# The gather of a deformable convolution: all row units sent by DMA over two queues, weights by one clamp in place

## What is computed

```python
def _deform(x, ow, ob):
    off = (_conv(x, ow, 1) + ob[None, :, None, None]).reshape(B, C, 2, H, W)
    py = jnp.clip(yy + off[:, :, 0], 0.0, H - 1)
    px = jnp.clip(xx + off[:, :, 1], 0.0, W - 1)
    y0, x0 = floor(py), floor(px);  y1, x1 = min(y0 + 1, H - 1), min(x0 + 1, W - 1)
    wy, wx = py - y0, px - x0
    return v00*(1-wy)*(1-wx) + v01*(1-wy)*wx + v10*wy*(1-wx) + v11*wy*wx
h = _deform(x, ow1, ob1);  h = _bn(_conv(h, w1, 0), g1, b1, m1, v1)
h = _deform(h, ow2, ob2);  h = _bn(_conv(h, w2, 1), g2, b2, m2, v2)
h = _deform(h, ow3, ob3);  h = _bn(_conv(h, w3, 0), g3, b3, m3, v3)
```

## Time and profile before

| | |
|---|---|
| Three runs | 5919.41, 5877.91, 5885.14 us; median 5885.14 |
| Profiled execution, span | 5921.8 us (no separate time beside it is on record) |
| TensorE busy, instructions | 5032.9 us (85%), 30592 |
| VectorE | 3610.3 us (61%), 4317 |
| ScalarE | 1856.8 us (31%), 2899 |
| GpSimd | 1464.4 us (25%), 1828 |
| SyncE's queue of the 16 DMA engines | 271640 packets, 533.13 MB, 36.3% |

### The profile page before, as it was taken

One profiled execution on the slowest core, in us unless ns is written; L12 is line 12 of the kernel. 1 busy time (PEld: TensorE's weight loads), 2 busy tenths in 40 slices (PEclk: granted clock), 3 DMA queues, 4 the chain that ended last, 5 costly groups with the idle time before them and its releaser, 6 DMA issues. The chain is left out here.

```text
span 5921.8 us, 79668 instructions
## 1 busy us (share of the span) xinstructions
PE 5032.9 (85%) x30592; PEld 2727.3 (46%) x30592; DVE 3610.3 (61%) x4317; ACT 1856.8 (31%) x2899; POOL 1464.4 (25%) x1828
## 2 busy tenths in 40 slices
PE   4877877876999799997998995999999967986987
PEld 2333333324777677766776772222222233232222
DVE  6888878885666566653222223767677765653764
ACT  2222222202222122210000003667677743641750
POOL 0222222230000000002001002555555543442540
PEclk7888888867999899998999997889799887777987
DMA  1000000001000000002211216889899968857962
GB/s 30 15 15 22 22 22 22 15 15 72 15 15 8 22 1 14 15 19 100 68 61 65 75 50 153 205 196 211 181 219 216 210 171 174 185 121 137 215 172 92
DMA packets 272018, 538.25 MB, mean 91 GB/s; under 512 B 167976, under 2 KB 169576, under 8 KB 264728
## 3 DMA queue, kind: packets, MB, share of 16 engines
q1 hardware_dynamic: 271640, 533.13, 36.3%
HBM read 419.75 MB, written 113.25 MB: 90 GB/s over the span
## 5 line engine op out<-in xcount | busy, mean ns | idle before, releaser
L1436 POOL TENSOR_SCALAR g_kw<-g_kw 128x512 f32<-128x512 f32 x1536 | 947.0, 641 | 904.3 <-ACT g_kw L1422 666.3
L1422 ACT ACTIVATE g_vw<-ps,l_index 128x512 f32<-128x512 f32 x1536 | 970.0, 685 | 409.5 <-PE ps L1478 409.4
L1455 DVE SCALAR_TENSOR_TENSOR g_prod<-g_vw,ps 128x1024 f32<-128x1024 f32 x768 | 902.7, 1217 | 271.4 <-PE ps L1493 270.8
L1296 PE MATMUL ps<-o_pad,o_ow 128*128 128x512 f32 x3456 | 851.8, 408 | 8.4 <-DVE o_pad L822 7.7
L1478 PE MATMUL ps<-g_coord,l_spread 80*128 80x512 f32 x1920 | 743.2, 489 | 125.2 <-DMA g_coord<-coords 125.1
L1093 PE MATMUL ps<-l_pair,l_w 128*128 128x512 f32 x3072 | 779.8, 403 | 0.0
L1478 PEld LDWEIGHTS ps<-g_coord,l_spread 80*128 80x128 f32 x1920 | 343.2, 213 | 906.3 <-ACT g_vw L1422 679.6
L1296 PEld LDWEIGHTS ps<-o_pad,o_ow 128*128 128x128 f32 x3456 | 656.8, 191 | 197.9 <-DVE o_pad L822 7.9
L1093 PEld LDWEIGHTS ps<-l_pair,l_w 128*128 128x128 f32 x3072 | 575.7, 191 | 156.4 <-issue 29.4
L1422 ACT ACTIVATE g_kw<-ps,l_index 128x512 f32<-128x512 f32 x384 | 264.3, 688 | 1176.3 <-PE ps L1478 1162.1
L1493 PE MATMUL ps<-g_kw,g_img 32*32 32x512 f32 x12288 | 508.9, 687 | 126.2 <-DVE g_prod L1455 100.0
(11 more groups left out here) (247 smaller groups left out, 4737.7 us busy)
## 6 DMA issues: line engine op xcount, KB each, us to landing
g_rows<-whole SPq DMA_DIRECT2D x1536, 192.0 KB, 4.9
coords<-o_parts SPq DMA_DIRECT2D x32, 1024.0 KB, 4.0
g_coord<-coords SPq DMA_DIRECT2D x96, 256.0 KB
l_x<-xcur SPq DMA_DIRECT2D x16, 1024.0 KB, 6.1
coords<-o_parts SPq DMA_DIRECT2D x32, 512.0 KB, 5.6
g_img<-dense SPq DMA_DIRECT2D x96, 128.0 KB, 4.4
gathered<-g_res SPq DMA_DIRECT2D x48, 256.0 KB, 4.7
l_xn<-in_x SPq DMA_DIRECT2D x8, 1024.0 KB, 5.0
```

The lines of the kernel that those rows point to most:

```text
L1296: ins = nc.tensor.matmul(ps[:, lo:lo + HALF], ow[:, a, kk, tap, y, k * P:(k + 1) * P], padded_rows(pad[:, m, c, kk], j, tap), start=(n == ...
L1422: nc.scalar.activation(to, bank(a % RING), ACT.Relu, bias=index[:, 0:1]).then_inc(sem("ring_read"), 1)
L1436: nc.gpsimd.tensor_scalar(part, part, 1.0, 0.0, ALU.min, ALU.max).then_inc(sem("clamped"), 1)
L1455: nc.vector.scalar_tensor_tensor(prod[:, n % PB, 2 * half:2 * half + 2, :].rearrange("p r n -> p (r n)"), vw[:, n % VB, 2 * half:2 * half ...
```

## The change

In each turn the y positions of all four channels of a unit are sent by DMA, 8 KB a partition, so the fifth spread matmul, its ScalarE pass and the loads of row coordinates go. Blocks 0 and 1 are sent from SyncE's queue, blocks 2 and 3 from GpSimd's. There are five buffers for rows, and a buffer is free when the row matmuls that read it have ended. The weights are made in place: instead of clamp(y - i + 1, 0, 1) a partition holds clamp(y, i - 1, i), with both limits from a column `clamp`, on GpSimd for channel 0 and on VectorE for the others. The constant i - 1 that is left over in each weight is made up for in image row 0, whose weight is always 1: `ramp_base` computes what has to stand there in the offset blocks. The positions of y no longer need splitting.

```diff
+def ramp_base(nc, link, out, rows):
+    link(nc.vector.tensor_reduce(out, rows[:, 0:SIDE - 1, :].rearrange("p y w -> p w y"), AX, ALU.add))
+    return nc.vector.scalar_tensor_tensor(out, rows[:, SIDE - 1, :], -float(SIDE - 2), out, ALU.mult, ALU.add)
@@ Coordinates.vector
         link(stt(pos, off, bias, grid, ALU.add, ALU.add))
-        link(ts(pos, pos, 0.0, float(SIDE - 1), ALU.max, ALU.min))
+        clipped = ts(pos, pos, 0.0, float(SIDE - 1), ALU.max, ALU.min)
+        if columns is None:
+            return clipped
@@ build_gather
-        KB, VB, PB, SB = 3, 2, 2, 3
+        VB, PB, SB = 2, 2, 5
+        def send_row(eng, q, r, half):
+            s, j, g = quads[q]
+            lo = r * SIDE + 4 * g
+            eng.dma_start(rows[r * SIDE:(r + 1) * SIDE, q % SB].rearrange("p c n -> p (c n)"),
+                          whole[s, j, lo:lo + 4].rearrange("q n -> (q n)").partition_broadcast(SIDE))\
+               .then_inc(sem(f"{half}_rows_sent{q % SB}"), 16)
@@ SyncE
-                        sp.wait_ge(sem("sent_relu"), q - SB + 1)
-                    for r in (0, 2, 1, 3):
+                        sp.wait_ge(sem("rows_summed"), q - SB + 1)
+                    for r in range(2):
+                        send_row(sp, q, r, "even")
-                def load_rows(s):
@@ GpSimd
-                    for c in range(4):
-                        ...
-                        nc.gpsimd.tensor_scalar(part, part, 1.0, 0.0, ALU.min, ALU.max).then_inc(sem("clamped"), 1)
+                nc.gpsimd.memset(coord[CM:CROWS, :, :, :].bitcast(F32), 0.0).then_inc(sem("coord_zero"), 1)
+                pool.wait_ge(sem("coord_zero"), 1)
+                for q in range(SB):
+                    send_odd(q)
+                for q in range(Q):
+                    await_rows(pool, q)
+                    part = rows[:, q % SB, 0, :]
+                    nc.gpsimd.tensor_scalar(part, part, clamp[:, 0:1], clamp[:, 1:2], ALU.max,
+                                            ALU.min).then_inc(sem("first_clamped"), 1)
+                    if q + SB - 2 >= SB and q + SB - 2 < Q:
+                        send_odd(q + SB - 2)
@@ VectorE
+                def clamp_rows(q):
+                    await_rows(dve, q)
+                    part = rows[:, q % SB, 1:4, :].rearrange("p c n -> p (c n)")
+                    nc.vector.tensor_scalar(part, part, clamp[:, 0:1], clamp[:, 1:2], ALU.max,
+                                            ALU.min).then_inc(sem("rest_clamped"), 1)
@@ build_offsets_1, for each image and channel half
+                            link(ramp_base(nc, link, base[:, m % 2, k, :], xm[:, k, :].rearrange("p (y w) -> p y w", w=SIDE)))
```

More of the change, by code:

```diff
@@ L1312, in build_gather @@
         sem = st.sem
[L1313 to L1314 removed]
+        spread, fold, index, clamp = (consts[name] for name in ("spread", "fold", "index", "clamp"))
+        VB, PB, SB = 2, 2, 5
         coord = st.sb("coord", [CROWS, 2, 4, N], F32R)
[L1316 to L1317 removed]
+        img = st.sb("img", [P, 2, QUADS, 4, SIDE])
+        rows = st.sb("rows", [P, SB, 4, HALF])
         vw = st.sb("vw", [P, VB, 4, HALF])
```

206 lines of the change are left out of this document (91 added, 115 removed).

## The result

The kernel after takes 6102.4 us (median of 4 runs, 6086.6 to 6112.5); the kernel before, run beside it, 5902.3 us (median of 4, 5877.9 to 5949.3). The ratio is 1.033, with a 95% interval of 1.028 to 1.038: the change makes the kernel slower. The median lies 17 us above the range of the prediction (5615 to 6085 us). The profiled execution took 6112.5 us with a span of 6110.8, 189 us more than the span of before.

What follows compares the result with a forecast made beforehand. The gathers' 3.82 us turn and late rows, limited by the written partition band, were taken as the bound. Rows sent -152, gather starts +6 and offset blocks +7 gave -139 us from 5885.14: 5746 us, range 5615 to 6085.

Steps and rivals of the forecast that it cites:

- What bounds the kernel: Gathers: a turn can't fall under 3.82 us; the other 299 us are late rows and half-clock turns after them.
- Step 1: Rows sent in the gathers: 16.78 MB a set at 313 GB/s, 66 us a set, -152 us.
- 270 GB/s as the lower end: Rate of the rows sent if the second queue brings nothing; the upper end was 426 GB/s.
- the 13.25 GB/s an engine: Rate of one half of the partitions (212/16), from which 313 GB/s for the rows sent was worked out.
- the picture itself: Rows sent: some 2.65 KB a block pass under the next block's transfer, since partition halves use different ports.
- Rival (b): Gathers slower: the same 270 GB/s with a third more bytes, 5986 us; chance 0.22.
- 32 reads of one row: Sign of being wrong: row rate set by repeated reads of the same memory row, not the written band's width.
- Step 2: Fifth spread matmul and ScalarE pass leave each turn: nothing at full clock; half-clock turns take 5.97 us.
- Step 3: GpSimd in the gathers: one clamp and two DMA issues of 1 us, 2.6 of 3.82 us, hidden; costed at nothing.
- Rival (c): GpSimd becomes the gathers' bound: issues of 2.2 us make a turn 5.0 us, 6082 us; chance 0.13.
- Step 4: Each gather's start: memset before GpSimd's rows, +6 us in all; first matmul 17 to 24 us after first issue.
- Step 5: Offset blocks: ramp_base reduction of about 1.4 us, mostly under TensorE's convolutions in the first block; +7 us.

Runs made afterwards that it cites:

- e18: Kernel before with whole kept eight times in memory, sends onto 128 partitions, the next set's loads spread, and five row buffers in place of three: 5795 us, ratio 0.977.
- e4: None of the kernel's work: nine stretches of sends alone in different partition patterns, queues and source rows, then clamps; 230 GB/s for blocks 0, 2, 1, 3 from one queue.
- e5: None of the kernel's work: five stretches of sends onto 128 partitions from 16, 8, 4, 16 and 32 different rows, then clamp forms; 225 GB/s for 16, 422 for 32.
- e11: Kernel after with GpSimd's clamp taking the minimum first and then the maximum: 6089 us, ratio 1.024.
- e1: Kernel after with the clamp of channel 0 moved from GpSimd to VectorE: 6066 us, ratio 1.027.
- e2: Kernel after with GpSimd's clamp between two constants in place of two columns (channel 0 weighted wrongly): 6071 us, ratio 1.028.
- e6: Kernel after with the ramp_base steps of the first offset block moved behind the splits and coordinates: 6044 us, ratio 1.018.

## Why the prediction was wrong

**What bounds the kernel: right.** Undisturbed turns are 3.8 us in both kernels, and e18 shows that 61.1 us a set is reached as soon as rows are never late. The waits for rows were the loss before, and are a larger one now.

**Step 1, rows sent: the step that failed.** It put the rows at 313 GB/s, 53.6 us a set, and the sets at 66 us. The sets take 80 us, at 238 GB/s for everything that is moved; less the 12.2 us that the step gave to columns, image and stores, that leaves some 68 us for the rows, 248 GB/s. The error has three parts. First, 270 GB/s as the lower end was one window of 10 us; the mean of busy engines in the earlier trace rows is 229 to 234 GB/s, and stood in the rows that the prediction began with. By it the sum is 18.9 MB / 0.229 to 0.234 = 81 to 82 us a set, near the result. Second, the 212 GB/s for one half was read in 1.7 us at a busy share of only 0.76; that is 279 GB/s for busy engines, no less than the rows' 270/0.98 = 276, so the 13.25 GB/s an engine, and with it the 313, had no basis in that row. Third, the picture itself (part of a block passes under the next) isn't borne out: two queues alone gave at most 276 GB/s in e4, and 16 groups over all partitions 225 in e5.

**Rival (b)** had the mechanism, the same rate with a third more bytes; its price was 5986 because it took 270 too (and 76 us a set where its own sum says 76.6). With the 235 GB/s of after its sum, 24 x 80.3 + 30 = 1957 us, is 191 over the 1766, so 5885 + 191 + 13 = 6089 us, within 0.3% of the result. That closeness is in part luck: the gathers grew by 150 us, not 191, and the first offset block, for which this sum has next to nothing, by 36. The 0.22 that I gave it was too little for the view that the rows favoured. What I named as making me wrong, 32 reads of one row, plays next to no part (230 against 235 GB/s in e4).

**Step 2** was near in the half-clock turn: 6.11 us where 5.97 were forecast, after 6.54.

**Step 3, GpSimd: right that the issue is hidden, wrong in the clamp.** The issue costs 0.54 us where I took 1. The clamps with limits from columns were "costed at nothing"; VectorE's grew from 1.01 to 1.08 us, but GpSimd's from 0.61 to 2.68, mostly because the diff also turned minimum and maximum round (1.23 in e11, where they stand as before). In the time it cost at most some 1%: e1, e2 and e11 gained 0.5 to 0.9%, each with an interval that overlaps that of after. Rival (c) with its issues of 2.2 us didn't happen. The Trainium skill (SBUF — State Buffer, "A bandwidth-pool intuition that's wrong (but worth ruling out)") tells of a DMA from GpSimd that took 3100 ns beside a VectorE copy. Here the issue stayed at 0.54 us in the mean, and GpSimd's sends landed after 10.0 us, SyncE's after 12.0; no run sets them apart from VectorE's clamps.

**Step 4, the start: near in the sum, wrong in the sign that it named.** The first matmul came 13.9 us after the first issue, not 17 to 24 (18.9 before), since the columns were there sooner. But the first row matmul, behind the memset and GpSimd's sends, came at 24.6 us against 23.0: +1.6 us in the first gather and +1.0 in each of the others, 3.6 us where 6 were forecast.

**Step 5, the offset blocks: wrong in place and size.** +7 us were forecast and +35 measured. The reduction takes 1.94 us and the small step 0.19, 2.1 us together where 1.4 were taken; that it reads its rows with a stride may be why, no run tells. More important, in the first block it isn't "otherwise under TensorE's convolutions": it stands on VectorE ahead of coordinates for which TensorE's next offsets wait (`coords_ready`), up to 4.6 us, six times. e6 gives all of the block's 36 us back. The middle blocks, for which the step had 5.6 us less 1.7, have not grown (+0.9 and -2.4 us); whether the stores saved pay for the reduction there, no run separates.

## What to carry to other kernels

Take a rate from the widest window there is, bytes over busy time, and not from the best ten microseconds; look at the busy share beside each rate. Where transfers are the bound, more bytes cost time, and here a second queue didn't change that. Before more bytes are sent to save work, time the sends alone in the planned pattern of partitions: here a pattern found in two such runs (422 against 230 GB/s), with the clamp's order, the ramps' place and the loads mended, turned +3.3% into -2.9%. And when a diff swaps two operations of an instruction or moves work ahead of a hand-over, cost the instruction anew and ask who waits behind it.

## What the runs showed of the hardware

- Sends of 8 KB a partition onto 128 partitions, by the number of groups of equal rows, from SyncE: 4 groups 106 GB/s at a share of 0.25, 8 groups 125 to 213 at 0.5, 16 groups 225 at 1.0, 32 groups 422, 128 different rows 423 (e4, e5). 4 groups from GpSimd: 110 GB/s at 0.93.
- Sends onto blocks of 32 partitions: 220 GB/s in the order 0, 1, 2, 3; 230 in 0, 2, 1, 3; 248 in the latter with 6 KB a partition; 240 with the halves on SyncE and ScalarE, 271 on SyncE and GpSimd (e4).
- GpSimd's clamp of 128x512 numbers with constants, in a row and with the gaps between: 0.68 us with the minimum first, 1.99 with the maximum first; one minimum alone, with no second operation, 1.56 us (9.34 us for six). VectorE's clamp of 128x1536 takes 0.96 us in either order (e5).
- A DMA issue on GpSimd: 0.49 us at the least, 0.54 in the mean (after).
